# GNN stack on one core: the first layer's normalising spread over three engines, and the residual additions of two passes moved from VectorE to GpSimd

## The chip, the cores and the metric

The kernel runs on one core of one Trainium2 chip. The metric is the device time of one execution in microseconds, the median of several. Engines are named as in the profile: PE (TensorE, matmuls), PEld (its weight loads), DVE (VectorE), ACT (ScalarE), POOL (GpSimd), SP (SyncE, which only issues DMAs here). They run side by side and are ordered by semaphores alone.

## What is computed

Four graph layers on x (4096 nodes, 128 features) and one adjacency matrix adj (4096 x 4096, fp32, 64 MB). Each layer normalises x, multiplies by the adjacency matrix and adds its result to x:

```
h = relu(layernorm(x)); x = x + norm(adj) @ h @ W_in + norm(adj.T) @ h @ W_out   # layer 0
h = relu(layernorm(x)); x1 = silu(adj @ h @ W + b)
                        x = x + silu(adj @ x1 @ W + b)                           # layer 1
h = relu(layernorm(x)); x = x + relu(adj_n @ h @ W + b)                          # layer 2
h = relu(layernorm(x)); x = x + relu(adj_n @ h @ W + b)                          # layer 3
```

adj_n is (adj + I) scaled by 1/sqrt of the degrees on both sides.

## The kernel before

**Tiles and substeps.** x stays in SBUF (`x_sb`, 32 blocks of 128 nodes). The matrix is streamed from HBM in tiles of 128x1024 fp32 (512 KB). Each tile is one substep n, 768 in all: 256 for layer 0, which meets adj and its transpose together, then four passes ("sweeps" 1 to 4) of 128 substeps over adj.T: pass 1 and 2 are layer 1's two products, pass 3 is layer 2, pass 4 is layer 3.

**A substep.** To keep fp32 accuracy on PE's faster format, every operand is split into a rounded high part and a rest. For a tile, SP loads it into `raw` (a ring of 10 places, in the passes 14, the last four in `acc`); ACT writes the high part `a_hi` (`hi`, L410 and L412); DVE writes the rest `a_lo` = raw - a_hi (`lo`, L546, both inputs in SBUF); PE then does six matmuls of 512 columns: a_hi with the features' high and low part (L786), and one substep later a_lo with the high part (L794). `a_hi` and `a_lo` are rings of 8, in the passes 6. In layer 0 the places 6 and 7 lie in `h_hi` and `h_lo`, so rows there name these tensors. SP may load tile n only when DVE is through with tile n-10 (n-14).

**Order around it.** Each engine's program is a loop over n, written out by hand: tables that map n to further work say what an engine does behind its part of substep n. Every engine works strictly in its own order, so a wait holds up all that stands behind it.

**The first layer's features.** x's 32 blocks come in 10 parts (`FIRST`): parts 0 to 3 are two blocks each, the rest four. For each part: DVE takes mean and variance (`first_stats`, L552, L556), ACT the square root (`first_std`, L417), DVE the reciprocal and the bias -mean*rstd (`first_affine`, L562, L568), ACT normalises with relu (`first_relu`, L435) and writes the high part (L439), DVE the low part (`first_lo`). Part 0 goes another way: DVE subtracts and multiplies (L730), ACT takes relu and high part in one operation. PE needs part i (of 0 to 3) at substep 6i. `act_raw` is a scratch tile of four blocks that the parts use in turn, `stats0`, `std0`, `rstd0` lie in `zt`. Behind substeps 25 to 30 ACT also copies the first finished banks (`copy_partial`, L455), behind 32 it normalises part 4.

**The slots of a pass.** A pass's result for four blocks is worked into x in a slot of 14 substeps (passes 2 and 3, 8 slots each, which reach into the next pass). In slot order: ACT copies the bank (`prod_out`), PE multiplies by W, DVE adds the bias into `zt` (`z_out`, behind substep 5 of the slot in pass 2 and 6 in pass 3, there after ACT's scaling), then, in pass 2, ACT takes silu of `zt` (behind 7) and DVE adds it to x (`x_plus_silu`, L692, behind 8); in pass 3 DVE takes relu and adds in one operation right behind `z_out` (L686). DVE then takes the statistics (`ln_stats`, L592, L596, behind 8), and scale and bias (`ln_affine`) behind 11 (pass 2) or 13; ACT writes the next features behind 15 or 17, DVE their low part behind 16 or 18. In pass 2 the inverse root is GpSimd's (L391 and L394, on 4 columns); that and four small operations at the start are all its work. From pass 3's features on, DVE also adds the identity to the diagonal tiles ahead of time (`plus`, L538).

Of the kernel before, what the change touches and what calls it, by code (L numbers as in the profile page):

```python
# [7 lines left out]
ALU = mybir.AluOpType  # L8
# [7 lines left out]
def build_gnn_stack(nc, x, adj, adj_t, w_in, w_out, w1, b1, w2, b2, w3, b3, out):  # L16
# [22 lines left out]
    with ctx:  # L39
# [3 lines left out]
        def sem(name):  # L43
            return ctx.enter_context(nc.semaphore(name))
# [232 lines left out]
        PASS_Z = places({1: 5, 2: 5, 3: 6, 4: 5})  # L279
        PASS_SILU = places({1: 8, 2: 7})  # L280
        PASS_SCALE = places({3: 5})
        PASS_STATS = places({2: 8, 3: 8})
        PASS_STD = places({3: 12})
        PASS_AFFINE = places({2: 11, 3: 13})
        PASS_HI = places({1: 8, 2: 15, 3: 17})
        PASS_LO = places({1: 9, 2: 16, 3: 18})

# [27 lines left out]
        FIRST_STD = {3: 1, 8: 2, 13: 3, 28: 4, 40: 5, 54: 6, 68: 7, 81: 8, 94: 9}
        FIRST_AFFINE = {3: 1, 8: 2, 13: 3, 29: 4, 41: 5, 55: 6, 69: 7, 82: 8, 95: 9}
        FIRST_RELU = {4: 1, 9: 2, 14: 3, 32: 4, 44: 5, 58: 6, 71: 7, 84: 8, 97: 9}
        FIRST_LO = {4: 1, 10: 2, 15: 3, 33: 4, 45: 5, 59: 6, 72: 7, 85: 8, 98: 9}  # L320
# [14 lines left out]
        @block.sync  # L335
        def _(sp):

            def load_x(i):
                b0, b1 = FIRST[i] if i < 2 else (GB, CB) if i == 2 else ((i - 2) * CB, (i - 1) * CB)
                sp.dma_start(x_sb[:, b0:b1, :], x[:, b0:b1, :]).then_inc(x_in[i], 16)  # L340

            def load(n):
                source, g, k = substeps[n]
                tile = source[g, k // 2, :, k % 2, :]
                if raw_before[n] is not None:
                    sp.wait_ge(sub_lo, raw_before[n] + 1)
                elif n >= S0:
                    sp.wait_ge(z_ready, (z_col(1, 1), z_col(1, 1), z_row(2, 1), z_col(2, 1))[raw_place[n] - RAWS] + 1)
                sp.dma_start(sub_raw(n), tile).then_inc(tile_in[raw_place[n]], 16)  # L349

            load_x(0)
            for n in range(RAWS):
                load(n)
                if n in (2, 6):
                    load_x(1 if n == 2 else 2)
            weights = (w_in, w_out, w1, w2, w3)
            biases = (b1, b2, b3)
            for n in range(RAWS, len(substeps)):
                load(n)
                if n in LOAD_X:  # L360
                    load_x(LOAD_X[n])
                if n in LOAD_W:
                    i = LOAD_W[n]
                    sp.dma_start(w_sb[:, i, :], weights[i]).then_inc(const_in, 16)
                if n in LOAD_B:
                    i = LOAD_B[n]
                    sp.dma_start(b_sb[:, i, :], biases[i].rearrange("(a n) -> a n", a=1).to_broadcast([P, D]))\
                      .then_inc(const_in, 16)

            for q in range(NQ - 1):  # L370
                sp.wait_ge(x_upd, 2 * NQ + q + 1)
                sp.dma_start(out[:, GB * q:GB * q + GB, :], x_sb[:, GB * q:GB * q + GB, :]).then_inc(out_done, 16)
            for quarter in range(2):
                blocks = slice(GB * NQ - GB + 2 * quarter, GB * NQ - GB + 2 * quarter + 2)
                sp.wait_ge(x_upd, 3 * NQ + quarter)
                sp.dma_start(out[:, blocks, :], x_sb[:, blocks, :]).then_inc(out_done, 16)
            sp.wait_ge(out_done, 16 * (NQ + 1))

        @block.gpsimd
        def _(pool):  # L380
            pool.memset(eps_sb[:, :], EPS).then_inc(eps_made, 1)
            pool.memset(ident[:, :], 0.0).then_inc(ident_made, 1)
            pool.memset(minus_half[:, :], -0.5)
            pool.wait_ge(ident_made, 1)
            pool.affine_select(out=ident[:, :], in_=ident[:, :], compare_op=ALU.not_equal, fill=1.0,
                               base=0, pattern=[[-1, P]], channel_multiplier=1).then_inc(ident_made, 1)

            for q in range(NQ):
                n = LN_BEFORE[2] + q
                pool.wait_ge(mv_ready, n + 1)  # L390
                pool.tensor_tensor(std[:, :], mv[:, :, 1], eps_sb[:, :].to_broadcast([P, GB]), ALU.add)\  # L391
                    .then_inc(std_ready, 1)
                pool.wait_ge(std_ready, n + 1)
                pool.tensor_tensor(rstd[:, :], std[:, :], minus_half[:, :].to_broadcast([P, GB]), ALU.pow)\  # L394
                    .then_inc(rstd_ready, 1)

        @block.scalar
        def _(act):
# [25 lines left out]
            def split_hi(sweep, q):  # L424
# [2 lines left out]
                act.activation(h_hi[SET_OF[sweep]][:, GB * q:GB * q + GB, :],  # L427
                               act_raw[:, :].rearrange("p (b f) -> p b f", b=GB), ACT.Copy).then_inc(h_hi_ready, 1)

            def first_relu(i):  # L430
                b0, b1 = FIRST[i]
                act.wait_ge(bias0_ready, i)
                act.wait_ge(h_ready, i)
                for n in range(b0, b1):
                    last = act.activation(act_raw[:, n % GB * D:(n % GB + 1) * D], x_sb[:, n, :], ACT.Relu,  # L435
                                          bias=bias0[:, n:n + 1], scale=rstd0[:, n:n + 1])
                last.then_inc(act_ready, 1)
                act.wait_ge(act_ready, i + 1)
                act.activation(h_hi[0][:, b0:b1, :], act_blocks(b0, b1), ACT.Copy).then_inc(h_hi_ready, 1)  # L439
# [40 lines left out]
            def first_layer(n):  # L480
                if n in FIRST_STD:
                    first_std(FIRST_STD[n])
                if n in FIRST_RELU:
                    first_relu(FIRST_RELU[n])
                if n in DRAIN and runs[DRAIN[n][0]][2] == 0:
                    copy_partial(*DRAIN[n])
                if n in STD:
                    ln_std(0, STD[n])
                if n in RELU:
                    ln_relu(0, RELU[n])  # L490
                if n == DSQ[1]:
                    act.wait_ge(dsq_ready, 1)
                    act.activation(d_isqrt[:, :], d_isqrt[:, :], ACT.Sqrt).then_inc(dsq_ready, 1)

            first_std(0)
            act.wait_ge(act_ready, 1)
            act.activation(h_hi[0][:, 0:2, :], act_blocks(0, 2), ACT.Relu).then_inc(h_hi_ready, 1)
            for n in range(S0):
                _, kind, d, k, _, _ = seq[n]
                hi(n, deg_part[:, 1 - kind, k, d:d + 1])  # L500
# [30 lines left out]
        def _(dve):  # L531
# [27 lines left out]
            def first_rstd(i):  # L559
# [11 lines left out]
            def first_lo(i):  # L571
                b0, b1 = FIRST[i]
                dve.wait_ge(h_hi_ready, i + 1)
                if i == 0:
                    dve.scalar_tensor_tensor(out=h_lo[0][:, b0:b1, :], in0=act_blocks(b0, b1), scalar=0.0,  # L575
                                             in1=h_hi[0][:, b0:b1, :].bitcast(F32), op0=ALU.max, op1=ALU.subtract)\
                       .then_inc(h_ready, 1)
# [83 lines left out]
            def z_out(sweep, q):  # L661
# [19 lines left out]
                                                       scalar=d_isqrt[:, GB * q + b:GB * q + b + 1],  # L681
                                                       in1=b_sb[:, B_OF[sweep], :], op0=ALU.mult, op1=ALU.add)
                ins.then_inc(zt_ready, 1)
                if sweep in (3, 4):
                    dve.wait_ge(zt_ready, zi - 16 + 1)
                    dve.scalar_tensor_tensor(out=x_sb[:, GB * q:GB * q + GB, :], in0=zt4, scalar=0.0,  # L686
                                             in1=x_sb[:, GB * q:GB * q + GB, :], op0=ALU.max, op1=ALU.add)\
                       .then_inc(x_upd, 1)

            def x_plus_silu(q):  # L690
                dve.wait_ge(silu_ready, q + 1)
                dve.tensor_tensor(x_sb[:, GB * q:GB * q + GB, :], zt[:, :].rearrange("p (b f) -> p b f", b=GB),  # L692
                                  x_sb[:, GB * q:GB * q + GB, :], ALU.add).then_inc(x_upd, 1)
# [35 lines left out]
            for n in range(2):
                last = dve.tensor_scalar(act_raw[:, n * D:(n + 1) * D], x_sb[:, n, :], mv0[:, n, 0:1],  # L730
                                         rstd0[:, n:n + 1], ALU.subtract, ALU.mult)
            last.then_inc(act_ready, 1)
# [5 lines left out]
            for n in range(S0, len(substeps)):  # L738
# [195 lines left out]
```

## Time and profile before

| | |
|---|---|
| time, median of 3 runs | 1110.21 us (1110.18 to 1110.29) |
| profiled execution | 1110.27 us, span 1108.1 us |
| PE busy | 1093.3 us (99%) |
| DVE busy | 1044.0 us (94%) |
| ACT busy | 913.9 us (82%) |
| POOL busy | 24.4 us (2%) |
| DMA | 408.40 MB, mean 369 GB/s |

The span is what the profile's rows are timed in; the device time holds 2.2 us more. Busy is the union of an engine's instructions. Instructions of one engine overlap a little in the records, so a group's count times its mean can exceed the time that the group really takes; where it matters, the spacing of starts is used. "Idle before" is the time in which the engine stood still in front of an instruction, and "<-" names what ended it.

### The profile page before, as it was taken

How to read it: one execution, taken by the hardware profiler on the slowest of the kernel's cores; microseconds unless marked ns; L12 is line 12 of the kernel's file. 1: busy time of each engine (PE TensorE's matmuls, PEld its weight loads, DVE VectorE, ACT ScalarE, POOL GpSimd, SP SyncE). 2: the span in 40 equal slices, each digit the busy share in tenths (PEclk: the TensorE clock that was granted, in tenths of full speed). 3: DMA queues.
4: the chain of work that ended last, by engine and by line, in shares of the span. 5: the costliest groups of instructions: out<-in, count | busy, mean ns of one | idle time of the engine just before them, and what ended most of it. 6: DMA issues, size and time to landing. Idle time of an engine off the chain costs nothing.

```text
span 1108.1 us, 15462 instructions
## 1 busy us (share of the span) xinstructions
PE 1093.3 (99%) x4992; PEld 909.4 (82%) x4992; DVE 1044.0 (94%) x1431; ACT 913.9 (82%) x1320; POOL 24.4 (2%) x24
## 2 busy tenths in 40 slices
PE   6999999999999999999999999999999999999998
PEld 5788888888888888888888888888888888888886
DVE  6999999999899999989989899999989999999987
ACT  7999998799779588878877788888888988887774
POOL 0000000000000000000000012111100000000000
PEclk9999999999999999999999999999999999999999
DMA  9999999999999899999999999999999999999993
GB/s 348 408 407 401 402 382 378 353 391 410 357 357 357 304 409 410 409 409 380 343 363 408 381 329 372 369 358 370 359 399 349 368 357 355 379 368 410 372 342 120
DMA packets 113984, 408.40 MB, mean 369 GB/s; under 512 B 12656, under 2 KB 14192, under 8 KB 113904
## 3 DMA queue, kind: packets, MB, share of 16 engines
q1 hardware_dynamic: 113904, 407.42, 96.5%
q8 instruction: 39, 0.64, 0.2%
q14 instruction: 41, 0.34, 0.1%
HBM read 405.27 MB, written 2.10 MB: 368 GB/s over the span
## 4 chain that ended last, share of the span: by engine, by line
PE 95%; DVE 2%; ACT 2%; issue 1%; DMA 1%; SPq 0%; ACTq 0%; DVEq 0%
PE bank L786 60%; PE bank L794 30%; PE bank L819 4%; DVE a_lo L546 1%; DMA raw<-in_adj_t_dram 1%; ACT a_hi L412 1%; ACT act_raw L435 0%; PE bank L809 0%; DVE h_lo L546 0%; ACT acc L455 0%; PE bank L811 0%; ACT h_hi L412 0%; DVE zt L762 0%; DVE x_sb L767 0%; SPq L349 0%
## 5 line engine op out<-in xcount | busy, mean ns | idle before, releaser
L546 DVE TENSOR_TENSOR a_lo<-raw,a_hi 128x1024 fp32r<-128x1024 f32 x560 | 657.4, 1220 | 34.1 <-ACT a_hi L410 15.6
L786 PE MATMUL bank<-a_hi,h_hi 128*128 128x512 f32 x1400 | 437.4, 394 | 8.7 <-ACT a_hi L412 8.7
L794 PE MATMUL bank<-a_lo,h_hi 128*128 128x512 f32 x1400 | 432.2, 390 | 0.6 <-DVE a_lo L546 0.6
L786 PE MATMUL bank<-a_hi,h_lo 128*128 128x512 f32 x1400 | 432.5, 390 | 0.0
L410 ACT ACTIVATE a_hi<-raw 128x1024 fp32r<-128x1024 f32 x368 | 374.1, 1054 | 56.7 <-PE bank L786 42.5
L786 PEld LDWEIGHTS bank<-a_hi,h_hi 128*128 128x128 f32 x1400 | 259.7, 188 | 61.7 <-DVE h_lo L575 6.5
L794 PEld LDWEIGHTS bank<-a_lo,h_hi 128*128 128x128 f32 x1400 | 263.4, 188 | 56.2 <-DVE a_lo L546 1.5
L786 PEld LDWEIGHTS bank<-a_hi,h_lo 128*128 128x128 f32 x1400 | 263.6, 188 | 55.0
L412 ACT ACTIVATE a_hi<-raw 128x1024 fp32r<-128x1024 f32 x192 | 201.4, 1052 | 17.1 <-PE bank L786 4.9
L546 DVE TENSOR_TENSOR a_lo<-acc,a_hi 128x1024 fp32r<-128x1024 f32 x144 | 170.9, 1217 | 4.2 <-ACT a_hi L410 1.9
L410 ACT ACTIVATE a_hi<-acc 128x1024 fp32r<-128x1024 f32 x144 | 145.2, 1057 | 15.3 <-PE bank L786 14.2
L546 DVE TENSOR_TENSOR h_lo<-raw,h_hi 128x1024 fp32r<-128x1024 f32 x64 | 76.3, 1219 | 1.8 <-ACT h_hi L412 1.8
L412 ACT ACTIVATE h_hi<-raw 128x1024 fp32r<-128x1024 f32 x64 | 67.3, 1053 | 4.6 <-DMA raw<-in_adj_dram 1.5
L445 ACT ACTIVATE act_raw<-x_sb,lnbias,lnscale 128x128 f32<-128x128 f32 x96 | 39.6, 483 | 18.0 <-DVE lnbias L624 17.8
L786 PE MATMUL bank<-h_hi 128*128 128x512 f32 x128 | 39.7, 391 | 1.2 <-ACT h_hi L412 1.2
L786 PE MATMUL bank<-h_hi,h_lo 128*128 128x512 f32 x128 | 39.5, 390 | 0.0
L794 PE MATMUL bank<-h_lo,h_hi 128*128 128x512 f32 x128 | 39.5, 390 | 0.0
L819 PEld LDWEIGHTS bank<-w_sb,prod_t 128*128 128x128 f32 x280 | 36.6, 191 | 2.7
L819 PE MATMUL bank<-w_sb,prod_t 128*128 128x128 f32 x280 | 36.8, 275 | 0.0
L412 ACT ACTIVATION_READ_ACCUMULATOR a_hi<-raw 128x1 f32 x192 | 35.8, 186 | 0.0
L460 ACT ACTIVATE prod_t<-bank 128x512 f32<-128x512 f32 x30 | 17.4, 582 | 20.3 <-PE bank L794 20.3
L786 PEld LDWEIGHTS bank<-h_hi 128*128 128x128 f32 x128 | 23.9, 188 | 6.5 <-ACT h_hi L412 1.6
(78 smaller groups left out, 391.9 us busy)
## 6 DMA issues: line engine op xcount, KB each, us to landing
raw<-in_adj_t_dram SPq DMA_DIRECT2D x496, 512.0 KB, 6.8
acc<-in_adj_t_dram SPq DMA_DIRECT2D x144, 512.0 KB, 6.4
raw<-in_adj_dram SPq DMA_DIRECT2D x128, 512.0 KB, 7.2
out_dram<-x_sb SPq DMA_DIRECT2D x7, 256.0 KB, 5.8
x_sb<-in_x_dram SPq DMA_DIRECT2D x3, 512.0 KB, 8.8
x_sb<-in_x_dram SPq DMA_DIRECT2D x2, 128.0 KB, 4.9
x_sb<-in_x_dram SPq DMA_DIRECT2D x1, 256.0 KB, 10.0
out_dram<-x_sb SPq DMA_DIRECT2D x2, 128.0 KB, 1.7
```

The costliest lines, as they stand in the source:

```text
L410: act.activation(sub_hi_of(n), sub_raw(n), ACT.Copy).then_inc(sub_hi, 1)
L412: act.activation(sub_hi_of(n), sub_raw(n), ACT.Copy, accum_out=accum).then_inc(sub_hi, 1)
L445: last = act.activation(act_raw[:, b * D:(b + 1) * D], x_sb[:, GB * q + b, :], ACT.Relu, bias=lnbias[:, b:b + 1], scale=lnscale[:, b:b + 1])
L460: act.activation(prod_t[:, half, :], banks_of(sweep, g)[half][:, :], ACT.Copy).then_inc(prod_ready, 1)
L546: dve.tensor_tensor(sub_lo_of(n), sub_raw(n), sub_hi_of(n).bitcast(F32), ALU.subtract).then_inc(sub_lo, 1)
L786: last = pe.matmul(bank[half][:, :], weights, sub_hi_of(n)[:, half * GW:(half + 1) * GW], start=start and weights is hi_w, stop=False)
L794: last = pe.matmul(bank[half][:, :], hi_w, sub_lo_of(n)[:, half * GW:(half + 1) * GW], start=False, stop=stop)
L819: last = pe.matmul(z_ps[half][:, b * D:(b + 1) * D], src[:, b * P:(b + 1) * P], w_sb[:, w, :], start=True, stop=True)
```

## The change

Two things, in one edit.

1. In layer 0, parts 1 to 3 are now made like part 0: subtract and multiply first (`first_norm`), then relu and high part in one operation on ACT (`first_hi`). Part 1's subtraction is DVE's, that of parts 2 and 3 is GpSimd's. Statistics, roots and reciprocals of parts 1 to 3 stand at earlier substeps, and x's transfers for them are issued behind tiles 1 and 4 instead of 2 and 6. Parts 4 to 9 are as before.
2. In pass 2 GpSimd adds silu(z) to x. In pass 3 GpSimd takes relu of z in place and adds it to x, in two operations with a semaphore (`relu_ready`) between them. DVE waits for x_upd before the statistics, which stand one substep later, as does all that follows them in the slot.

```diff
-        PASS_STATS = places({2: 8, 3: 8})
-        PASS_STD = places({3: 12})
-        PASS_AFFINE = places({2: 11, 3: 13})
-        PASS_HI = places({1: 8, 2: 15, 3: 17})
-        PASS_LO = places({1: 9, 2: 16, 3: 18})
+        PASS_STATS = places({2: 9, 3: 9})
+        PASS_STD = places({3: 13})
+        PASS_AFFINE = places({2: 12, 3: 14})
+        PASS_HI = places({1: 8, 2: 16, 3: 18})
+        PASS_LO = places({1: 9, 2: 17, 3: 19})
...
-        FIRST_STATS = {2: 1, 6: 2, 11: 3, 24: 4, 36: 5, 50: 6, 64: 7, 77: 8, 90: 9}
+        FIRST_STATS = {1: 1, 4: 2, 7: 3, 24: 4, 36: 5, 50: 6, 64: 7, 77: 8, 90: 9}
...
-                if n in (2, 6):
-                    load_x(1 if n == 2 else 2)
+                if n in (1, 4):
+                    load_x(1 if n == 1 else 2)
...
+            for i in (2, 3):
+                pool.wait_ge(rstd0_ready, i + 1)
+                pool.wait_ge(h_ready, i - 1)
+                for n in range(*FIRST[i]):
+                    last = pool.tensor_scalar(act_raw[:, n % GB * D:(n % GB + 1) * D], x_sb[:, n, :], mv0[:, n, 0:1],
+                                              rstd0[:, n:n + 1], ALU.subtract, ALU.mult)
+                last.then_inc(act_ready, 1)
...
+            for sweep in (2, 3):
+                for q in range(NQ):
+                    x4 = x_sb[:, GB * q:GB * q + GB, :]
+                    zt4 = zt[:, :].rearrange("p (b f) -> p b f", b=GB)
+                    if sweep == 2:
+                        pool.wait_ge(silu_ready, q + 1)
+                        pool.tensor_tensor(x4, zt4, x4, ALU.add).then_inc(x_upd, 1)
+                        ln_root(q)
+                    else:
+                        pool.wait_ge(zt_ready, z_of(sweep, q) - 16 + 1)
+                        pool.tensor_scalar(zt4, zt4, 0.0, None, ALU.max).then_inc(relu_ready, 1)
+                        pool.wait_ge(relu_ready, q + 1)
+                        pool.tensor_tensor(x4, zt4, x4, ALU.add).then_inc(x_upd, 1)
...
+            def first_hi(i):
+                b0, b1 = FIRST[i]
+                act.wait_ge(act_ready, i + 1)
+                act.activation(h_hi[0][:, b0:b1, :], act_blocks(b0, b1), ACT.Relu).then_inc(h_hi_ready, 1)
...
-                if sweep in (3, 4):
+                if sweep == 4:
                     dve.wait_ge(zt_ready, zi - 16 + 1)
                     dve.scalar_tensor_tensor(out=x_sb[:, GB * q:GB * q + GB, :], in0=zt4, scalar=0.0,
                                              in1=x_sb[:, GB * q:GB * q + GB, :], op0=ALU.max, op1=ALU.add)\
                        .then_inc(x_upd, 1)
...
-                    if sweep == 2:
-                        x_plus_silu(q)
                     dve.wait_ge(x_upd, (sweep - 2) * NQ + q + 1)
                     ln_stats(sweep, q)
```

ACT between its tiles 4 and 15 of layer 0; before (L412 tiles, L417 roots, L435 and L439 normalising, where ACT waits for DVE's bias):

```order
L412 ACTIVATE a_hi,deg_part<-raw 128x1024
L412 ACTIVATE h_hi,deg_part<-raw 128x1024 x2
L412 ACTIVATE a_hi,deg_part<-raw 128x1024
L417 ACTIVATE zt<-zt,eps_sb 128x2
L412 ACTIVATE a_hi,deg_part<-raw 128x1024
L435 ACTIVATE act_raw<-x_sb,zt 128x128 x2
L439 ACTIVATE h_hi<-act_raw 128x256
```

and after (L438 tiles, L443 roots, L459 relu and high part):

```order
L438 ACTIVATE h_hi,deg_part<-raw 128x1024
L438 ACTIVATE a_hi,deg_part<-raw 128x1024 x2
L443 ACTIVATE zt<-zt,eps_sb 128x2
L438 ACTIVATE a_hi,deg_part<-raw 128x1024
L459 ACTIVATE h_hi<-act_raw 128x256
L438 ACTIVATE a_hi,deg_part<-raw 128x1024 x3
```

The pair of L435 is gone, and the one activation that is left waits for GpSimd instead of for the bias.

DVE in one slot of pass 2, before (L673 writes zt, L692 adds to x, L592 and L596 are the statistics):

```order
L673 TENSOR_TENSOR zt<-bank,b_sb 128x512
L546 TENSOR_TENSOR a_lo<-raw,a_hi 128x1024 x2
L546 TENSOR_TENSOR a_lo<-acc,a_hi 128x1024
L692 TENSOR_TENSOR x_sb<-zt,x_sb 128x512
L592 BN_STATS stats<-x_sb 128x6 x4
L596 BN_AGGR mv<-stats 128x2 x4
```

and after:

```order
L711 TENSOR_TENSOR zt<-bank,b_sb 128x512
L578 TENSOR_TENSOR a_lo<-raw,a_hi 128x1024 x2
L578 TENSOR_TENSOR a_lo<-acc,a_hi 128x1024 x2
L630 BN_STATS stats<-x_sb 128x6 x4
L634 BN_AGGR mv<-stats 128x2 x4
```

L692 has left the engine; four tiles instead of three stand ahead of the statistics, which now wait for GpSimd.

GpSimd at the end of pass 2 and in pass 3; before, it has only the small operations of pass 2 and then nothing:

```order
L391 TENSOR_TENSOR std<-mv,eps_sb 128x4
L394 TENSOR_TENSOR rstd<-std,minus_half 128x4
```

after, with the last slot of pass 2 and two of pass 3 (L415 is pass 2's addition, L419 relu, L421 pass 3's addition):

```order
L415 TENSOR_TENSOR x_sb<-zt,x_sb 128x512
L403 TENSOR_TENSOR std<-mv,eps_sb 128x4
L406 TENSOR_TENSOR rstd<-std,minus_half 128x4
L419 TENSOR_SCALAR zt<-zt 128x512
L421 TENSOR_TENSOR x_sb<-zt,x_sb 128x512
L419 TENSOR_SCALAR zt<-zt 128x512
L421 TENSOR_TENSOR x_sb<-zt,x_sb 128x512
```

Everything of 512 columns is new on this engine.

## Rows read from the trace of the kernel before

Tile names in these rows: `bank` a PSUM bank, `zt`, `x_sb`, `raw`, `acc`, `a_hi`, `a_lo` as above.

**Rows 1.** The page: part 1, and one group of part 5 (mean ns).
```profile
PE 1093.3 (99%) x4992; PEld 909.4 (82%) x4992; DVE 1044.0 (94%) x1431; ACT 913.9 (82%) x1320; POOL 24.4 (2%) x24
...
L546 DVE TENSOR_TENSOR a_lo<-raw,a_hi 128x1024 fp32r<-128x1024 f32 x560 | 657.4, 1220 | 34.1 <-ACT a_hi L410 15.6
```

**Rows 2.** Waits of PE, 0 to 36 us: us in total, times, longest.
```profile
PE bank L786 <- ACT a_hi L412: 8.5, 4, 6.6
PE bank L786 <- ACT h_hi L412: 1.2, 1, 1.2
```

**Rows 3.** PE in order of time: start us, us, what, [idle before].
```profile
31.24 0.61 PE L794 MATMUL bank<-a_lo,h_hi 128*128 128x512 f32 x2
...
33.08 0.73 PE L786 MATMUL bank<-h_hi 128*128 128x512 f32 x2 [1.23 <-ACT h_hi L412]
...
56.78 0.62 PE L786 MATMUL bank<-a_hi,h_lo 128*128 128x512 f32 x2
57.24 0.61 PE L794 MATMUL bank<-h_lo,h_hi 128*128 128x512 f32 x2
58.05 0.73 PE L786 MATMUL bank<-a_hi,h_hi 128*128 128x512 f32 x2 [0.20 <-ACT a_hi L412]
```

**Rows 4.** ScalarE in order of time.
```profile
30.66 0.88 ACT L435 ACTIVATE act_raw<-x_sb,zt 128x128 f32<-128x128 f32 x2 [1.18 <-DVE zt L568]
...
42.30 1.04 ACT L412 ACTIVATE a_hi<-raw 128x1024 fp32r<-128x1024 f32 x1
...
44.29 0.60 ACT L455 ACTIVATE acc<-bank 128x512 f32<-128x512 f32 x1 [0.85 <-PE bank L794]
```

**Rows 5.** Windows: busy us of each engine, clock, DMA share, GB/s.
```profile
10.00:44.30 34.30, 31.16 (x130) 24.36 (x130) 29.71 (x44) 29.81 (x61) 0.00 (x0) 1.00 1.03 409
44.30:57.90 13.60, 13.55 (x60) 10.89 (x58) 11.28 (x19) 13.57 (x28) 0.00 (x0) 1.00 1.03 410
```

**Rows 6.** Line 349 (tile loads), the one issue between 33.9 and 34.7 us.
```profile
L349 SPq DMA_DIRECT2D raw<-in_adj_dram x1: 328/328/328, 34.3 to 34.3; - x1
...
DMA to landing us min/median/max: 7.8/7.8/7.8
```

**Rows 7.** Waits of PE, 900 to 1000 us.
```profile
PE bank L794 <- DVE a_lo L546: 0.6, 2, 0.4
```

**Rows 8.** PE in order of time, third pass.
```profile
970.39 0.61 PE L786 MATMUL bank<-a_hi,h_lo 128*128 128x512 f32 x2
971.41 0.73 PE L794 MATMUL bank<-a_lo,h_hi 128*128 128x512 f32 x2 [0.40 <-DVE a_lo L546]
```

**Rows 9.** VectorE in order of time: a slot of pass 2, one of pass 3.
```profile
643.38 0.69 DVE L692 TENSOR_TENSOR x_sb<-zt,x_sb 128x512 f32<-128x512 f32 x1
644.10 0.87 DVE L592 BATCH_NORM_STATS2 stats<-x_sb 128x6 f32<-128x128 f32 x4
...
645.31 3.46 DVE L546 TENSOR_TENSOR a_lo<-acc,a_hi 128x1024 fp32r<-128x1024 f32 x3
...
843.11 0.69 DVE L686 SCALAR_TENSOR_TENSOR x_sb<-zt,x_sb 128x512 f32<-128x512 f32 x1
843.72 0.29 DVE L538 TENSOR_TENSOR raw<-raw,ident 128x128 f32<-128x128 f32 x1
```

**Rows 10.** GpSimd in order of time.
```profile
0.73 0.10 POOL L381 MEMSET eps_sb<- 128x1 f32 x1 [0.29 <-POOLq L923]
...
1.21 0.29 POOL L385 TENSOR_SCALAR_AFFINE_SELECT ident<-ident 128x128 f32<-128x128 f32 x1 [0.20 <-POOL ident L382]
645.48 1.08 POOL L391 TENSOR_TENSOR std<-mv,eps_sb 128x4 f32<-128x4 f32 x1 [643.98 <-DVE mv L596]
646.64 1.88 POOL L394 TENSOR_TENSOR rstd<-std,minus_half 128x4 f32<-128x4 f32 x1
```

**Rows 11.** Windows, most of pass 2 (columns as in rows 5).
```profile
640.00:787.00 147.00, 147.00 (x679) 122.79 (x678) 145.97 (x240) 125.92 (x155) 21.30 (x15) 1.00 0.98 362
```

**Rows 12.** Waits of VectorE, 640 to 975 us.
```profile
DVE a_lo L546 <- ACT a_hi L410: 3.1, 2, 2.5
```

More of the change, by code:

```diff
@@ L106, in build_gnn_stack @@
         silu_ready = sem("silu_ready")
+        relu_ready = sem("relu_ready")
         scaled_ready = sem("scaled_ready")
@@ L236, in build_gnn_stack @@
                 plus_cols[n] = slice(k % CB * P, (k % CB + 1) * P)
+        NORMED = 4
         FIRST = [(b, b + GB // 2) for b in range(0, CB, GB // 2)] + [(GB * q, GB * q + GB) for q in range(2, NQ)]
@@ L313, in build_gnn_stack @@
         DSQ = (S0 + 64, S0 + 67, S0 + 70)
-        FIRST_STATS = {2: 1, 6: 2, 11: 3, 24: 4, 36: 5, 50: 6, 64: 7, 77: 8, 90: 9}
[L317 to L320, printed above, removed]
+        FIRST_STATS = {1: 1, 4: 2, 7: 3, 24: 4, 36: 5, 50: 6, 64: 7, 77: 8, 90: 9}
+        FIRST_STD = {2: 1, 6: 2, 9: 3, 28: 4, 40: 5, 54: 6, 68: 7, 81: 8, 94: 9}
+        FIRST_RSTD = {2: 1, 5: 2, 8: 3}
+        FIRST_AFFINE = {29: 4, 41: 5, 55: 6, 69: 7, 82: 8, 95: 9}
+        FIRST_HI = {4: 1, 10: 2, 14: 3}
+        FIRST_RELU = {32: 4, 44: 5, 58: 6, 71: 7, 84: 8, 97: 9}
+        FIRST_LO = {4: 1, 10: 2, 14: 3, 33: 4, 45: 5, 59: 6, 72: 7, 85: 8, 98: 9}
         def banks_of(sweep, g):
@@ L386, in _, with ln_root @@
                                base=0, pattern=[[-1, P]], channel_multiplier=1).then_inc(ident_made, 1)
-            for q in range(NQ):
+            for i in (2, 3):
[5 more added lines that the diff above has]
+                last.then_inc(act_ready, 1)
+            def ln_root(q):
                 n = LN_BEFORE[2] + q
@@ L428, in split_hi @@
                                act_raw[:, :].rearrange("p (b f) -> p b f", b=GB), ACT.Copy).then_inc(h_hi_ready, 1)
+            def first_hi(i):
+                b0, b1 = FIRST[i]
+                act.wait_ge(act_ready, i + 1)
+                act.activation(h_hi[0][:, b0:b1, :], act_blocks(b0, b1), ACT.Relu).then_inc(h_hi_ready, 1)
             def first_relu(i):
                 b0, b1 = FIRST[i]
-                act.wait_ge(bias0_ready, i)
+                act.wait_ge(bias0_ready, i - NORMED + 1)
                 act.wait_ge(h_ready, i)
@@ L482, in first_layer @@
                     first_std(FIRST_STD[n])
+                if n in FIRST_HI:
+                    first_hi(FIRST_HI[n])
                 if n in FIRST_RELU:
@@ L495, in _ @@
             first_std(0)
-            act.wait_ge(act_ready, 1)
-            act.activation(h_hi[0][:, 0:2, :], act_blocks(0, 2), ACT.Relu).then_inc(h_hi_ready, 1)
+            first_hi(0)
             for n in range(S0):
@@ L563, in first_rstd, with first_norm @@
                 dve.wait_ge(rstd0_ready, i + 1)
+            def first_norm(i):
+                for n in range(*FIRST[i]):
+                    last = dve.tensor_scalar(act_raw[:, n % GB * D:(n % GB + 1) * D], x_sb[:, n, :], mv0[:, n, 0:1],
+                                             rstd0[:, n:n + 1], ALU.subtract, ALU.mult)
+                last.then_inc(act_ready, 1)
             def first_affine(i):
@@ L573, in first_lo @@
                 dve.wait_ge(h_hi_ready, i + 1)
-                if i == 0:
+                if i < NORMED:
                     dve.scalar_tensor_tensor(out=h_lo[0][:, b0:b1, :], in0=act_blocks(b0, b1), scalar=0.0,
@@ L688, in z_out @@
                        .then_inc(x_upd, 1)
[L690 to L693, printed above, removed]
             def first_layer(n):
@@ L699, in first_layer @@
                     first_stats(FIRST_STATS[n])
+                if n in FIRST_RSTD:
+                    i = FIRST_RSTD[n]
+                    first_rstd(i)
+                    if i == 1:
+                        first_norm(i)
                 if n in FIRST_AFFINE:
@@ L728, in _ @@
             first_rstd(0)
[L729 to L732, printed above, removed]
+            first_norm(0)
             first_lo(0)
```

## The prediction

> **What bounds the kernel now.** I read the page's first part, then PE's waits, then the engines in order of time wherever PE waited. PE is busy 1093.3 of 1108.1 us and DVE 1044.0 [rows 1]. So there is little to win: only PE's waits and what stands before its first matmul. The reader should look for three places.
>
> First the start. PE waits four times for ScalarE's first half of a tile: 8.5 us less the 6.6 before its first matmul, and once 1.2 [rows 2]. From start to start it costs more: the pair of matmuls at 31.24 should be followed after 0.45 (as 56.78 is by 57.24) and is followed after 1.84, and the pair behind the wait takes 0.11 longer [rows 3], so 1.5 us for this one. The column gives this wait as 1.23 idle, so each wait costs some 0.27 more than its idle time, and the four, 1.9 + 1.2 = 3.1 us idle, about 4.2. ScalarE is late there because it waits in front of its normalising work for VectorE's bias (1.18 us at 30.66), behind which the next tiles queue [rows 4].
>
> Second, one wait at 58.05: 0.20 idle, 0.47 from start to start [rows 3]. ScalarE is busy 13.57 of the 13.6 us before it [rows 5].
>
> Third, two waits for VectorE in the third pass: 0.6 idle together [rows 7], the larger 1.02 - 0.45 + 0.11 = 0.68 from start to start, the two about 1.1 [rows 8]. From 640 us on VectorE is nearly full: 145.97 of 147 us [rows 11], and in the whole stretch to 975 it waits 3.1 us [rows 12]. PE is on time there only because VectorE had run ahead.
>
> **The start: spread parts.** Statistics of parts 1 to 3 come one to four substeps earlier, x's two small transfers stand one and two tiles earlier on SP's queue, and the normalising leaves ScalarE for VectorE (part 1) and GpSimd (parts 2, 3). ScalarE loses six activations of about 0.44 us [rows 4] and, more important, the waits for the bias. The price: tile 2 comes behind 128 KB of x and tiles 5 and 6 behind 256 KB, at 409 GB/s [rows 5] 0.3 and 0.6 us; these eat into the gain of the first tiles but not into what is left at 58 us (below). VectorE gains two tensor_scalars and loses three small operations for the bias, about even. I take the four waits as mostly gone by the 22nd tile: up to 4.2 us.
>
> But it doesn't last. ScalarE copies the first finished banks at 44.29, after waiting 0.85 for PE, and then has no pause until the wait at 58.05 [rows 4, 5]. If PE is earlier, ScalarE cannot copy before the tile in front: that tile's load was issued at 34.3 and landed 7.8 us later, at 42.1 [rows 6], and an earlier issue doesn't help, since the DMA engines are at a share of 1.03 throughout [rows 5]. ScalarE took it at 42.30 [rows 4], so it can start 0.2 us earlier, and the copy about 43.3, 1.0 us earlier than 44.29. From there the chain to 58.05 is as long as before: the start is worth -1.0 us at 58 us, whatever PE gained before. Bounds: 0 (the first tiles come late instead) and -4.2 (the copies are no chain). A slip of GpSimd's four small tensor_scalars costs nothing while it is under a tile or two, as parts 2 and 3 are wanted six tiles later.
>
> **The passes: what leaves VectorE.** In each of 8 slots of pass 2 the addition goes: 643.38 to 644.10, 0.72 us. In pass 3 the fused relu and addition goes: 843.11 to 843.72, 0.61 [rows 9]; the operation in front no longer has to be waited for, another 0.1. So 16 x 0.72 = 11.5 us less on VectorE. Nothing is taken from PE directly; if that were all, the two waits of the third pass would go: -1.1 us.
>
> **What GpSimd adds.** 8 additions of 128x512 in pass 2; 8 relus and 8 additions of that size in pass 3. The trace has no such operation. Nearest rows: a 128x128 operation with one input takes 0.29 us, a 128x1 memset 0.10 [rows 10], so 0.19 / 128 = 1.5 ns a column and 0.10 fixed; 512 columns with one input 0.10 + 0.77 = 0.87 us. Two inputs: between 0.87 (read side by side) and 0.10 + 2 x 0.77 = 1.64 (one after the other); I take the middle, 1.25.
>
> **Do they run beside VectorE?** This decides the case. While GpSimd has them, VectorE's queue holds only subtractions of 128x1024 with two inputs in SBUF: 3 or 4 of them stand between writing zt and the moved statistics. The one evidence is the pair of small operations that GpSimd has now. The first takes 1.08 us for four columns, and starting at 645.48 it ends at 646.56, just behind the first subtraction, which began at 645.31 and runs about 1.2 by its mean [rows 1, 9, 10]. All 8 do so. That is how an operation looks that may read only when VectorE's instruction is over. Against it: the second, 1.88 us long, delays no subtraction (three in 3.46 us: 1.2 and two steps of 1.13) [rows 9, 10]. But eight words of reading can slip between two instructions, 512 columns can't. I take it that the two exclude each other while both read, so GpSimd's time comes onto VectorE's, whoever waits: either the subtraction waits, or GpSimd does, and then VectorE stands at its wait for x_upd in front of the statistics. Behind that wait all subtractions queue, and PE needs those.
>
> The Trainium skill says it outright: SBUF — State Buffer, section "Who interferes with whom", has a VectorE instruction with two SBUF inputs contend with a GpSimd instruction that reads SBUF, by a lock held for the whole instruction. By that rule the time is the one of my sum; if the trace's undelayed subtractions under the second operation are taken as no contention at all, it is the first rival's. GPSIMD Engine Reference, section 3.1, gives 4497 ns for an addition of 2048 columns; a quarter, 1.12 us, is an estimate from that page, and with it the sum would be 1119.5.
>
> **Sum.** Pass 2, each slot: 1.25 - 0.72 = +0.53, 8 times +4.2. Pass 3: 0.87 + 1.25 - 0.72 = +1.40, 8 times +11.2. VectorE: +15.4 us. Its waits of 3.1 us take up that much; and since PE already waits for VectorE at 971 us, all the rest arrives at PE: +12.3. With the start: +12.3 - 1.0 = +11.3. The profiled run took 1110.27 (span 1108.1 and 2.2 around it), 0.06 over the median 1110.21: 1121.5 us. Its own range by the bounds of the addition: 0.87 gives 8 x 0.15 + 8 x 1.02 = 9.4, less 3.1, less 1.0: 1115.5; 1.64 gives 8 x 0.92 + 8 x 1.79 = 21.7, so 1127.9.
>
> Statistics one substep later cost nothing: 4 operations in another place. The second half of part 5 of the next pass's features is then done at the 17th or 19th substep behind the slot, still 5 and 3 tiles before PE wants it; its cover is that VectorE is never that far behind PE.
>
> **Rivals.**
> 1. No contention (faster side). GpSimd needs 2.1 us in pass 3 beside three subtractions, 3.4 us, so x_upd is there in time; the third pass's waits go. 1110.3 - 1.0 - 1.1 = 1108.1, and down to 1105 if more of the start's 4.2 lasts. For it: the undelayed subtractions. Against it: the ends at 646.56. It decides once a GpSimd operation costs VectorE less than about 0.4 us. 0.20.
> 2. No contention, but GpSimd is slow: its small operation's 1.08 us [rows 10] is a fixed cost. Then relu 1.9 and addition 2.6 need 4.5 us against 3.4; VectorE waits 1.1, net +0.4 in each slot of pass 3, 3.2 in all, which its 3.1 of pauses cover. Only the start is left: about 1109.3. 0.10.
> 3. Shared reading: VectorE loses not GpSimd's whole time but half of it or so. Pass 2: 0.63 - 0.72, pass 3: 1.06 - 0.72; in all +2.0, under the 3.1; up to +5.5 at two thirds. 1109 to 1112. 0.12.
> 4. The forecast, exclusion: 0.58.
>
> **How the numbers follow.** A measurement of this kernel can tell 0.2%, 2.2 us, from no change. Faster than 1108.0: half of rival 1 and little else, 0.12. Same: the rest of rival 1, rival 2, most of 3: 0.24. Slower: the forecast and the end of rival 3, 0.64. The likeliest is 1121.5 with its own range 1115.5 to 1127.9; for 8 in 10 the range must take in rivals 2 and 3 and the upper half of 1: 1107.9 to 1128.
>
> **What would show it.** Right: between 640 and 975 us the subtractions that overlap a GpSimd addition take 2 us or more instead of 1.22, or VectorE has idle time in front of its statistics put down to GpSimd's x_sb; PE's waits for a_lo in that stretch sum to over 10 us, with more of it in pass 3 than in pass 2; PE's busy share drops there alone. Start: no PE wait between 14 and 34 us over 0.5, and a wait before 58 us that has grown to some 2 us, since PE arrives 3 us earlier and ScalarE only 1. Wrong: subtractions at 1.22 beside GpSimd's long operations; GpSimd additions well under 0.87 or over 1.64 us; or the PE wait near 57 us not growing, which would mean that the start's whole gain is kept.

## The result, and the profile after

The changed kernel takes 1128.29 us, the median of 5 runs (1127.84 to 1128.88); the kernel before, timed beside it, takes 1110.29. The ratio is 1.0163 (95% interval 1.0152 to 1.0174): 18.0 us slower. The direction and the mechanism were those of the forecast, 1121.5 us, but the time is 6.8 us above it, and 0.3 us above the upper end of its range, 1128.0.

The page of the changed kernel, part 1, and from part 5 two of the three groups of GpSimd's new work in the passes (busy us in all, mean ns of one, idle before; the third, pass 3's addition L421, takes 1.30 us each time):

```profile
PE 1098.6 (98%) x4992; PEld 909.2 (81%) x4992; DVE 1038.0 (92%) x1414; ACT 912.4 (81%) x1314; POOL 119.5 (11%) x52
...
L415 POOL TENSOR_TENSOR x_sb<-zt,x_sb 128x512 f32<-128x512 f32 x8 | 36.8, 4604 | 689.7 <-ACT zt L509 689.7
...
L419 POOL TENSOR_SCALAR zt<-zt 128x512 f32<-128x512 f32 x8 | 36.7, 4583 | 145.9 <-DVE zt L715 145.9
```

Beside [rows 1]: VectorE did give up work, 1044.0 to 1038.0 us of it, and yet the kernel is slower. An addition or a relu of 512 columns shows as 4.6 us on GpSimd: so long it stands open, that is, from its recorded start to its end. The waits of the two passes, 640 to 993 us, say what that means (us in total, times, longest):

```profile
DVE stats L630 <- POOL x_sb L421: 19.4, 7, 2.8
...
PE bank L827 <- DVE a_lo L578: 13.8, 9, 3.0
...
DVE stats L630 <- POOL x_sb L415: 8.4, 7, 1.2
...
DVE a_lo L578 <- ACT a_hi L436: 1.5, 2, 0.9
```

VectorE, which waited 3.1 us there [rows 12], now stands 19.4 + 8.4 = 27.8 us in front of its statistics, and PE's waits for it have gone from 0.6 us [rows 7] to 13.8. In order of time, a slot of pass 2 and one of pass 3, VectorE first (start us, us, what, idle before):

```profile
659.58 2.35 DVE L578 TENSOR_TENSOR a_lo<-raw,a_hi 128x1024 fp32r<-128x1024 f32 x2
661.85 2.35 DVE L578 TENSOR_TENSOR a_lo<-acc,a_hi 128x1024 fp32r<-128x1024 f32 x2
665.39 0.87 DVE L630 BATCH_NORM_STATS2 stats<-x_sb 128x6 f32<-128x128 f32 x4 [1.19 <-POOL x_sb L415]
...
868.87 3.49 DVE L578 TENSOR_TENSOR a_lo<-acc,a_hi 128x1024 fp32r<-128x1024 f32 x3
875.13 0.87 DVE L630 BATCH_NORM_STATS2 stats<-x_sb 128x6 f32<-128x128 f32 x4 [2.77 <-POOL x_sb L421]
```

and GpSimd:

```profile
660.41 4.95 POOL L415 TENSOR_TENSOR x_sb<-zt,x_sb 128x512 f32<-128x512 f32 x1 [10.81 <-ACT zt L509]
...
869.04 4.67 POOL L419 TENSOR_SCALAR zt<-zt 128x512 f32<-128x512 f32 x1 [16.17 <-DVE zt L715]
873.79 1.30 POOL L421 TENSOR_TENSOR x_sb<-zt,x_sb 128x512 f32<-128x512 f32 x1
```

Four subtractions run from 659.58 to 664.20 at their usual step of 1.13 us, undelayed, with GpSimd's addition open from 660.41 on. It ends at 665.36, 1.16 us after the last of them. The relu, open from 869.04, ends at 873.71, 1.35 us after the third subtraction's end (868.87 + 3.49 = 872.36); the addition behind it, with VectorE standing still, takes 1.30. So GpSimd is shut out while VectorE runs one subtraction behind the other, and does its whole work once VectorE stands at the wait for that very work. Seven of eight slots in each pass are so. In the first slot of each pass GpSimd got in at the border between two subtractions instead, and VectorE was held up: its two from 639.53 take 3.46 us, not 2.35, and its three from 825.32 take 5.05, not 3.49.

At the start (PE, 0 to 60 us):

```profile
55.68 0.61 PE L827 MATMUL bank<-h_lo,h_hi 128*128 128x512 f32 x2
57.55 0.73 PE L819 MATMUL bank<-a_hi,h_hi 128*128 128x512 f32 x2 [1.25 <-ACT a_hi L438]
```

The wait before 58 us has grown from 0.20 to 1.25, and the matmul behind it starts 0.50 us earlier than in [rows 3].

### The profile page after: what moved, and what is told of

Read it like the earlier page. It is cut to its first block, busy times and chain, and to the rows that moved or that the text cites. A ratio compares the mean times of both kernels' runs of the same rounds, so it can differ in the third digit from the quotient of the medians.

```text
span 1125.8 us, 15467 instructions
## 1 busy us (share of the span) xinstructions
PE 1098.6 (98%) x4992; PEld 909.2 (81%) x4992; DVE 1038.0 (92%) x1414; ACT 912.4 (81%) x1314; POOL 119.5 (11%) x52
## 4 chain that ended last, share of the span: by engine, by line
PE 82%; DVE 8%; POOL 5%; issue 2%; DMA 2%; ACT 1%; SPq 0%; POOLq 0%; DVEq 0%; ACTq 0%
PE bank L819 52%; PE bank L827 26%; DVE a_lo L578 5%; PE bank L852 3%; POOL zt L419 3%; DMA raw<-in_adj_t_dram 2%; POOL x_sb L415 1%; DVE stats L630 1%; POOL x_sb L421 1%; DVE zt L715 0%; DVE h_lo L578 0%; ACT a_hi L438 0%; PE bank L842 0%; DVE h_lo L623 0%; ACT act_raw L466 0%
## 5 line engine op out<-in xcount | busy, mean ns | idle before, releaser
L578 DVE TENSOR_TENSOR a_lo<-raw,a_hi 128x1024 fp32r<-128x1024 f32 x560 | 658.9, 1222 | 32.0 <-ACT a_hi L436 13.8
L827 PE MATMUL bank<-a_lo,h_hi 128*128 128x512 f32 x1400 | 433.7, 391 | 13.8 <-DVE a_lo L578 13.8
L438 ACT ACTIVATE a_hi<-raw 128x1024 fp32r<-128x1024 f32 x192 | 201.9, 1055 | 22.4 <-PE bank L819 7.1
L415 POOL TENSOR_TENSOR x_sb<-zt,x_sb 128x512 f32<-128x512 f32 x8 | 36.8, 4604 | 689.7 <-ACT zt L509 689.7
L438 ACT ACTIVATE h_hi<-raw 128x1024 fp32r<-128x1024 f32 x64 | 67.5, 1056 | 6.2 <-DMA raw<-in_adj_dram 1.3
L419 POOL TENSOR_SCALAR zt<-zt 128x512 f32<-128x512 f32 x8 | 36.7, 4583 | 145.9 <-DVE zt L715 145.9
L630 DVE BATCH_NORM_STATS2 stats<-x_sb 128x6 f32<-128x128 f32 x96 | 20.9, 281 | 27.7 <-POOL x_sb L421 19.4
```

What stands on the lines that cost most here:

```text
L415: pool.tensor_tensor(x4, zt4, x4, ALU.add).then_inc(x_upd, 1)
L419: pool.tensor_scalar(zt4, zt4, 0.0, None, ALU.max).then_inc(relu_ready, 1)
L438: act.activation(sub_hi_of(n), sub_raw(n), ACT.Copy, accum_out=accum).then_inc(sub_hi, 1)
L578: dve.tensor_tensor(sub_lo_of(n), sub_raw(n), sub_hi_of(n).bitcast(F32), ALU.subtract).then_inc(sub_lo, 1)
L630: last = dve.bn_stats(stats[:, b, :], x_sb[:, GB * q + b, :])
L827: last = pe.matmul(bank[half][:, :], hi_w, sub_lo_of(n)[:, half * GW:(half + 1) * GW], start=False, stop=stop)
```

## The experiments

The theory: GpSimd's operation and VectorE's two-input subtractions exclude each other, so the passes lose GpSimd's time. The rival: something else that came with the change, the later statistics or the new start, costs the time, or GpSimd is only slow by itself. Times are medians; "before" was timed again beside each of the three sets of runs: 1110.31, 1110.39 and 1110.19 us.

**The change in parts.** Four kernels, each with the part named and the rest as before.

```diff
# start alone: the passes as before
-        PASS_STATS = places({2: 9, 3: 9})
+        PASS_STATS = places({2: 8, 3: 8})
# passes alone: GpSimd's loop over sweeps 2 and 3, start as before
# pass 2 alone, pass 3 alone: that sweep's branch only, and only its slots one substep later
+        PASS_STATS = places({2: 9, 3: 8})   # pass 2 alone
+        PASS_STATS = places({2: 8, 3: 9})   # pass 3 alone
```

The start alone. 

> The spread parts of layer 0 alone; passes 2 and 3 as before. My theory (the start's gain is cut to what ScalarE's chain from its first bank copy to 58 us gives, and GpSimd's four operations take 10.9 us there): the changed kernel's matmul that follows the wait near 58 us comes 0.5 us earlier than before (57.55 against 58.05), and nothing gives or takes after it, so 1109.8. Rival, the start is where some of the loss sits (GpSimd's slow operations disturb layer 0): 1111 or more. Rival, the start keeps all that the four waits cost: 1106.

Measured: 1109.48 us, ratio 0.9992 (0.9984 to 1.0001).

The passes alone. 

> GpSimd's work in passes 2 and 3 alone; layer 0 as before. My theory: all of the loss, 1128.3 + 0.5 = 1128.8. Rival, the start has a part in the loss: under 1127.5.

Measured: 1130.01 us, ratio 1.0174 (1.0160 to 1.0188).

Pass 2 alone. 

> Only pass 2's additions on GpSimd; pass 3 on VectorE as before, layer 0 as before. My theory (VectorE stands still 1.2 us a slot for an addition of 1.2 us, in place of its own 0.72): the waits of PE in pass 2 of the changed kernel, 2.6 us, are all of it: 1112.9. By the sum of the prediction (8 x 0.53 less 3.1 of pauses): 1111.4. Rival, GpSimd's operations disturb every VectorE operation: over 1116.

Measured: 1113.08 us, ratio 1.0025 (1.0015 to 1.0034).

Pass 3 alone. 

> Only pass 3's relus and additions on GpSimd; pass 2 on VectorE as before, layer 0 as before. My theory (VectorE stands still 2.8 us a slot for two operations, in place of its own 0.72): PE's waits in pass 3 of the changed kernel, 16.6, less the 1.1 of before: 1125.8. By the sum of the prediction (8 x 1.40 less 3.1): 1118.4.

Measured: 1126.6 us, ratio 1.0147 (1.0133 to 1.0160).

The parts add up to within 1 us: pass 2 and pass 3 give 2.8 + 16.3 = 19.1 against 19.7 for the passes together, and these 19.7 with the start's -0.8 give 18.9 against the whole change's 18.0. Closer they can't be compared: the executions of one kernel scatter by 1 to 3 us where pass 3's work is on GpSimd, and PE's clock, dealt with in the next section, has a part in it (granted 0.54 and 0.53 in two stretches of 3.4 us with the passes alone, 0.57 in one of 6.7 us with pass 3 alone). Six sevenths of the passes' loss is pass 3. Each part came out near its theory; the passes alone and pass 3 alone lost about 1 us more. VectorE's waits, 640 to 993 us, of pass 3 alone:

```profile
DVE stats L605 <- POOL x_sb L408: 16.6, 6, 2.8
DVE a_lo L559 <- ACT a_hi L423: 3.9, 3, 2.5
```

**The relu left out.** The changed kernel without GpSimd's relu in pass 3; its output lacks that relu.

```diff
-                        pool.tensor_scalar(zt4, zt4, 0.0, None, ALU.max).then_inc(relu_ready, 1)
-                        pool.wait_ge(relu_ready, q + 1)
```

> The changed kernel with pass 3's relu on GpSimd left out (x takes z without relu; the rest is the same), so GpSimd has one operation of two inputs in each slot of pass 3 instead of two. My theory (each GpSimd operation costs VectorE its own time, the relu with one input as much as the addition): VectorE's wait in a slot of pass 3 falls from 2.8 to 1.2 us, 8 x 1.5 = 12 us less on VectorE, PE's waits fall by about 11: 1117. Rival, the relu has only one input and costs the 0.87 us of the prediction: 8 x 0.9 = 7 us, 1121.

Measured: 1116.31 us, ratio 1.0051 (1.0036 to 1.0066). VectorE's waits:

```profile
DVE stats L628 <- POOL x_sb L415: 8.4, 7, 1.2
DVE stats L628 <- POOL x_sb L419: 8.4, 7, 1.2
```

An addition alone costs the same 1.2 us a slot in either pass, and the relu in front of it raised the seven waits from 8.4 to 19.4: 1.57 us each. In time it costs 18.0 - 5.9 = 12.1 us, two thirds of the whole loss, where the forecast had 8 x 0.87 = 7.0. Some 1.6 of the 12.1 us are PE's clock (next section), which stayed at 1.00 through the passes in this run; its longest wait of PE was 1.4 us.

**The statistics three substeps later still.** If GpSimd merely needs long, more subtractions beside it would hide it.

```diff
-        PASS_STATS = places({2: 9, 3: 9})
-        PASS_STD = places({3: 13})
-        PASS_AFFINE = places({2: 12, 3: 14})
+        PASS_STATS = places({2: 12, 3: 12})
+        PASS_STD = places({3: 16})
+        PASS_AFFINE = places({2: 15, 3: 17})
```

(The two `places` lines that are left out, for the features' high and low part, move three later too.) 

> The changed kernel with the statistics of passes 2 and 3, and all that follows them in the slot, three substeps later, so that seven (pass 2) or six (pass 3) subtractions stand between the writing of zt and the wait for x_upd, 6.8 us or more. My theory (GpSimd gets no turn while VectorE goes from one two-input operation straight to the next, and runs only when VectorE stands still): GpSimd's first operation of a slot grows by the same 3.4 us, to 8 us, VectorE's wait in front of the statistics stays 1.2 and 2.8 us, time 1128 give or take 2. Rival, GpSimd's operations take 4.6 and 1.3 us by themselves and VectorE is only there too early: the wait is gone, time 1109 to 1112.

Measured: 1120.68 us, ratio 1.0095 (1.0078 to 1.0112). Neither the theory's 1128 nor the rival's 1109 to 1112. The trace shows slots of two kinds. Here is one of each, VectorE:

```profile
659.12 1.22 DVE L578 TENSOR_TENSOR a_lo<-raw,a_hi 128x1024 fp32r<-128x1024 f32 x1
660.25 1.79 DVE L623 TENSOR_TENSOR h_lo<-act_raw,h_hi 128x512 fp32r<-128x512 f32 x1
...
742.06 0.69 DVE L623 TENSOR_TENSOR h_lo<-act_raw,h_hi 128x512 fp32r<-128x512 f32 x1
742.66 1.22 DVE L578 TENSOR_TENSOR a_lo<-raw,a_hi 128x1024 fp32r<-128x1024 f32 x1
743.80 4.63 DVE L578 TENSOR_TENSOR a_lo<-acc,a_hi 128x1024 fp32r<-128x1024 f32 x4
748.34 1.22 DVE L578 TENSOR_TENSOR a_lo<-raw,a_hi 128x1024 fp32r<-128x1024 f32 x1
750.75 0.87 DVE L630 BATCH_NORM_STATS2 stats<-x_sb 128x6 f32<-128x128 f32 x4 [1.19 <-POOL x_sb L415]
```

and GpSimd beside them:

```profile
659.95 1.54 POOL L415 TENSOR_TENSOR x_sb<-zt,x_sb 128x512 f32<-128x512 f32 x1 [6.80 <-ACT zt L509]
...
741.76 8.96 POOL L415 TENSOR_TENSOR x_sb<-zt,x_sb 128x512 f32<-128x512 f32 x1 [7.63 <-ACT zt L509]
```

At 741.76 GpSimd's addition opens and is shut out for nearly 8 us, while seven more of VectorE's operations start, and VectorE then waits the same 1.19 us as in the changed kernel, where three more started. So nothing of GpSimd's work gets done meanwhile, and a longer cover is worth nothing by itself. At 659.95 GpSimd gets in at VectorE's next change of instruction and is done in 1.54; VectorE pays with one operation of 1.79 instead of 0.69, 1.10 us. This is so in 6 slots of pass 2 and 5 of pass 3 (in the changed kernel in 1 and 1). In pass 3 a slot of this kind holds VectorE up by 0.42 under the relu and 1.12 under the addition, 1.54 together, against 2.77 when it is shut out. VectorE's loss is then 10.7 us of waits, 6 x 1.1 and 5 x 1.54: 25.0 us. In the changed kernel it was 27.8 + 1.1 + 1.56 = 30.5. This accounts for 5.5 of the 7.6 us between the two; the rest I can't place on VectorE. PE's own waits fell from 14.3 to 8.1 us (640 to 1020 us), and 2.3 of the 8.1 are one wait for `h_lo`: the first that the later slots cost.

What lets GpSimd in is open too: in both slots above it starts 0.30 us ahead of VectorE's next instruction. The relus of pass 3 in the two kernels give a clue, no more. Where one got in, VectorE ran close behind ScalarE: the half for its next subtraction was finished between 0.05 us before and 0.22 us after the relu's start, or VectorE had to wait for one (0.44 us, at 846.11). Where one was shut out, that half had been finished for 0.9 us or longer; but the slot at 931.26 goes against this.

**Work that nobody waits for.** The kernel before, with an extra addition (pass 2) or relu (pass 3) on GpSimd in each slot, which reads the weights and writes a spare tile in bf16; and the same with a memset in their place.

```diff
+                pool.wait_ge(silu_ready, q + 1)
+                pool.tensor_tensor(spare[:, :, :], w_sb[:, 0:4, :], w_sb[:, 0:4, :], ALU.add).then_inc(spare_ready, 1)
...
+                pool.wait_ge(zt_ready, z_of(3, q) - 16 + 1)
+                pool.tensor_scalar(spare[:, :, :], w_sb[:, 0:4, :], 0.0, None, ALU.max).then_inc(spare_ready, 1)
```

> The kernel before, with extra work on GpSimd that nobody waits for: in each slot of pass 2 an addition and in each slot of pass 3 a relu, of 128x512, reading the weights in SBUF and writing a tile that nothing reads (in bf16, half the bytes). The output is that of the kernel before. My theory (exclusion): the operation is stretched until VectorE's next stretch of one-input operations (bias add from PSUM, statistics), so 4 us and more where it would take 1.3; VectorE pays something each time GpSimd has its turn, in sum 2 to 8 us, of which PE sees 0 to 6: 1110.5 to 1116. Rival, slow by itself: 4.6 us each, VectorE untouched, 1110.3. Rival, no contention and fast: 1.3 us each, 1110.3.

Measured with the addition and the relu: 1114.0 us, ratio 1.0032 (1.0021 to 1.0044).

> As the run before, but each extra operation is a memset of the same tile: GpSimd writes and reads nothing. If what is contended is the reading of SBUF: each memset takes about as long as without VectorE (under 0.7 us), VectorE's subtractions keep 1.22 us, time 1110.3. Rival, any operation of GpSimd is stretched beside VectorE, or issuing on GpSimd is slow: memsets of 1 us and more, or a time above 1110.8.

Measured with the memset: 1110.68 us, ratio 1.0003 (0.9993 to 1.0012).

The spare addition and the spare relu on GpSimd:

```profile
661.50 4.16 POOL L394 TENSOR_TENSOR spare<-w_sb 128x512 bf16<-128x512 f32 x1 [11.95 <-ACT zt L488]
...
843.83 1.91 POOL L404 TENSOR_SCALAR spare<-w_sb 128x512 bf16<-128x512 f32 x1 [18.39 <-DVE zt L687]
```

and VectorE beside them:

```profile
662.93 1.23 DVE L556 TENSOR_TENSOR a_lo<-acc,a_hi 128x1024 fp32r<-128x1024 f32 x1
664.07 0.69 DVE L702 TENSOR_TENSOR x_sb<-zt,x_sb 128x512 f32<-128x512 f32 x1
664.79 0.87 DVE L602 BATCH_NORM_STATS2 stats<-x_sb 128x6 f32<-128x128 f32 x4
...
844.32 0.70 DVE L548 TENSOR_TENSOR raw<-raw,ident 128x128 f32<-128x128 f32 x1
```

VectorE's last operation with two inputs ends at 664.76, and the addition at 665.66, beside the statistics, which read one tile: it cost VectorE nothing, 7 times of 8. The relu got in every time, and held up the operation behind the border by 0.42 us (0.70 against the usual 0.28). That is 8 x 0.42 and once 0.85 in pass 2, 4.2 us, of which the pauses, down from 3.1 to 2.2 us, take 0.9: 3.3, against 3.6 measured. So there is a price for reading beside VectorE even where VectorE never waits for x_upd; writes don't have it, as the memset shows. One relu costs VectorE 0.42 us although GpSimd needs 1.35 for it when it runs alone.

**The start.** VectorE makes the subtractions of parts 2 and 3 too, passes as before; and in a second kernel, on top of that, part 4's relu and halves stand four substeps later, behind the wait at 57.5 us.

```diff
-            for i in (2, 3):
-                pool.wait_ge(rstd0_ready, i + 1)
...
-                    if i == 1:
-                        first_norm(i)
+                    first_norm(i)
...
-        FIRST_RELU = {32: 4, 44: 5, 58: 6, 71: 7, 84: 8, 97: 9}
+        FIRST_RELU = {36: 4, 44: 5, 58: 6, 71: 7, 84: 8, 97: 9}   # second kernel; FIRST_LO 33 -> 37
```

> The spread start with VectorE, not GpSimd, subtracting and multiplying for parts 2 and 3 too (four operations of about 0.3 us); passes as before. My theory (GpSimd's turn comes late in layer 0 as well, which cost PE waits at 29.5 and 34.4 us; but what the start keeps is set by ScalarE's chain from its first bank copy): no PE wait over 0.3 us between 14 and 34 us, the wait near 57 us grows by what the others shrink, and the matmul behind it still comes near 57.1 to 57.6: 1109.3 to 1109.8. Rival, ScalarE's chain is not the limit: 1107.5 or less.

Measured: 1109.24 us, ratio 0.9991 (0.9982 to 1.0000).

> The run before, and part 4's normalising on ScalarE behind substep 36 instead of 32 (its low part behind 37), so that these 2.2 us don't stand at the end of ScalarE's chain of bank copies. PE wants part 4 at substep 64. My theory: the wait near 57 us goes or falls under 1 us, and 1.0 to 1.5 us more of the start's gain are kept: 1108.0 to 1108.6, below both kernels. Rival, the transfers of the tiles are the limit there: no change against the run before.

Measured: 1109.44 us, ratio 0.9991 (0.9982 to 1.0000). The theory's 1108.0 to 1108.6 did not come; it is the rival's "no change". The relu's move did take away the wait at 57.5 us, but two smaller ones take its place:

```profile
35.30 0.70 PE L810 MATMUL bank<-a_hi,h_hi 128*128 128x512 f32 x2 [0.55 <-ACT a_hi L423]
...
73.43 0.73 PE L810 MATMUL bank<-a_hi,h_hi 128*128 128x512 f32 x2 [0.44 <-ACT a_hi L423]
```

ScalarE's waits for tiles to land sum to 6.3 us there up to 135 us, where before had 2.8: a part at least of what PE gained is lost again to the transfers. No kernel here beats the kernel before by more than 0.1%.

## Where the prediction was right, and the term that it mis-sized

- **The case.** Exclusion, and that VectorE would stand in front of its statistics with idle time put down to `x_sb`: right; rivals 1 to 3 fell with pass 3 alone at +16.3 us. PE's waits for `a_lo` came to over 10 us, with most of it in pass 3, as said; no wait of PE for `h_lo` appeared, so the later statistics seem to cost nothing by themselves (no run moves them alone). By the Trainium skill, SBUF — State Buffer, "Who interferes with whom", the two contend by a lock. The trace agrees for the addition where it got in, which costs VectorE 1.1 us of its 1.30; for the relu it does not, 0.42 of 1.35.
- **The addition, 1.25 us.** It measured 1.30 on a resting VectorE, and the wait it makes is 1.19. Pass 2 was sized right: its seven waits and one delay are 9.5 us, 8 x 1.25 would be 10.0. The estimate from the Trainium skill's GPSIMD Engine Reference, section 3.1, 1.12, is 0.2 under the trace.
- **The relu, 0.87 us: the step that failed.** I scaled a 128x128 affine_select of 0.29 us linearly to 512 columns. The relu takes 1.35 with VectorE at rest, as long as the addition with its two inputs, and in front of the addition it made VectorE's wait 1.57 longer. So "relu 0.87 + addition 1.25" = 2.12 a slot is 2.77 as waited, in seven slots; the first lost 1.56. With pass 2's 9.5, VectorE lost 30.5 us to GpSimd where the forecast had 8 x 1.25 + 8 x 2.12 = 27.0: +3.5 us. (The relu by itself is 7 x 0.70 = 4.9 over; the two first slots and the additions came out 1.4 under.) The upper bound of the range took 1.64 for the addition but left the relu at 0.87, with no end of its own.
- **The pauses, 3.1 us taken up.** Only 1.6 us of VectorE's 3.1 in [rows 12] were taken up; 1.5 remain. +1.5 us.
- **The start, -1.0 us at 58 us.** It is -0.5. The wait there grew, as said, but ScalarE's copy came at 43.80 instead of 43.3: the tile in front began at 42.74, not earlier than the 42.30 of [rows 4]. Its load was issued earlier (31.6 us) but took 11.1 us to land instead of the 7.8 of [rows 6]: 42.7, where it had been 42.1. The wait grew to 1.25 us, not to some 2. +0.5 us. GpSimd's four small operations there took 1.9 to 3.5 us each, beside VectorE; that cost nothing, as said: with VectorE doing them the time is the same (1109.24 against 1109.48).
- **Missing from the sum: PE's clock.** Windows of the changed kernel (length; busy us of PE, PEld, DVE, ACT, POOL; clock; DMA share; GB/s) just before, in and behind PE's longest wait in pass 3:

```profile
910.00:919.00 9.00, 9.00 (x41) 7.48 (x40) 7.01 (x11) 6.07 (x7) 5.83 (x2) 1.00 1.02 377
...
922.40:927.50 5.10, 5.07 (x15) 4.06 (x16) 5.10 (x8) 4.21 (x5) 0.00 (x0) 0.67 0.80 234
927.50:935.00 7.50, 7.50 (x39) 6.33 (x38) 7.43 (x14) 6.72 (x13) 0.00 (x0) 1.00 0.90 308
```

and the matmul behind the wait with the next that are slow:

```profile
922.43 0.74 PE L827 MATMUL bank<-a_lo,h_hi 128*128 128x512 f32 x2 [3.00 <-DVE a_lo L578]
923.01 0.63 PE L819 MATMUL bank<-a_hi,h_hi 128*128 128x512 f32 x2
923.48 0.77 PE L819 MATMUL bank<-a_hi,h_lo 128*128 128x512 f32 x2
924.05 1.05 PE L827 MATMUL bank<-a_lo,h_hi 128*128 128x512 f32 x2
```

PE stood 3.00 us, and then ran from 923.5 for some 3 us at the lower of its two levels, 1.2 GHz, with steps of 0.85 us instead of 0.45: some 1.6 us, which the forecast had no term for. It doesn't come each time: after the next wait of nearly this length, 2.94 us up to 990.49, the granted clock stayed at 1.00 in this trace (990.5 to 995.5 us), and with the passes alone it fell behind both.

- **The sum.** 1121.5 + 3.5 + 1.5 + 0.5 + 1.6 = 1128.6, against 1128.29. That it agrees to 0.3 us is partly luck, as executions of this kernel scatter by 1 us and the terms are no better known. The relu's term is the largest; since the range was missed by 0.3 us only, any one of the four, had it been in the sum and moved the range with it, would have brought the time inside.

## What to carry to other kernels

Handing elementwise work from a nearly full VectorE to an idle GpSimd did not pay here, where both read SBUF at the same time: GpSimd's 1.3 us were paid nearly whole by the engine meant to be relieved, and a fused operation that takes VectorE 0.7 us became two on GpSimd of 1.35 and 1.30. That nobody waits for the result lowers the price and doesn't remove it: the spare relus cost VectorE 0.42 us each. Placing the consumer later doesn't help by itself (8.96 us open, and the same 1.19 us of wait). What should help, though no run here tries it on the real additions, is to let GpSimd's work meet VectorE operations that don't exclude it: beside the statistics the spare addition was free. And a price scaled up from a smaller operation of another kind, as the relu's was, needs a bound of its own.

## What the runs showed of the hardware that I had not expected

- GpSimd can be shut out for very long: 8.96 us for an operation of 1.3, with seven VectorE operations started meanwhile. It isn't taken in turn.
- In other slots it gets in at once, and what tells the two kinds apart is open: the additions shown above start 0.30 us before VectorE's next instruction in both.
- A one-input operation of 512 columns takes GpSimd as long as a two-input one (1.35 and 1.30 us), but where it gets in between VectorE's operations it holds VectorE up by 0.42 us only, against 1.1. Where VectorE stands waiting for it, it costs the whole.
- A memset of 512 columns on GpSimd takes 0.52 us beside VectorE's subtractions and holds up nothing that the time shows (1110.68 against 1110.39 us):

```profile
L394 POOL MEMSET spare<- 128x512 bf16 x8 | 4.2, 525 | 725.6 <-ACT zt L488 725.6
```
